# Waiting for every pair of gathers in the attention loop of a four-layer graph network

## The reference

```python
h = (x @ W_att).reshape(n, H, D)
e = a_src[src] + a_dst[dst]
e = jnp.where(e > 0, e, SLOPE * e)
m = segment_max(e, dst)
e = jnp.exp(e - m[dst])
alpha = e / (segment_sum(e, dst)[dst] + SM_EPS)
out = segment_sum(alpha[:, :, None] * h[src], dst)
att_out = out.mean(axis=1) + bias_att
```

## Time and profile before

| | |
|---|---|
| median of the timed runs | 10293.0 us |
| span of the profiled execution | 10335.9 us |
| attention loop, first gather to the first instruction of the next block's gathers | 4321.5 to 7677.2 us |
| POOL busy, whole span | 5859.2 us (57%) |
| DVE busy | 5676.5 us (55%) |
| PE busy | 4876.0 us (47%) |
| gathers at L2099 | 1612, 1588.2 us busy |

### The profile page before, as it was taken

How to read it: one execution, slowest core, us unless ns; L and a number is a source line. 1 busy time by engine, 2 the same in 40 slices (tenths; PEclk the granted TensorE clock), 3 DMA queues, 4 the chain that set the end, 5 groups by cost and what they waited for, 6 DMA issues and landing times. The chain is left out here.

```text
span 10335.9 us, 115065 instructions
## 1 busy us (share of the span) xinstructions
PE 4876.0 (47%) x30691; PEld 3800.3 (37%) x30691; DVE 5676.5 (55%) x16123; ACT 2431.2 (24%) x4069; POOL 5859.2 (57%) x5314
## 2 busy tenths in 40 slices
PE   6888888884666666334444444444467000000000
PEld 3554455442556555234444444444465000000000
DVE  7888888885666666245555555555576212212221
ACT  0111111111333333134444444444453000000000
POOL 5888888884333333444444444444423666666665
PEclk8888888886777877555555555555555555555555
DMA  3333333332000000233333333333331111111111
GB/s 78 35 35 35 35 35 35 35 30 59 20 16 14 15 15 20 46 57 63 64 65 63 63 66 63 64 64 63 64 89 51 46 47 47 46 47 47 46 49 43
DMA packets 927382, 484.76 MB, mean 47 GB/s; under 512 B 828205, under 2 KB 842007, under 8 KB 925218
## 3 DMA queue, kind: packets, MB, share of 16 engines
q0 software_dynamic: 309120, 199.89, 16.7%
q1 hardware_dynamic: 615872, 277.33, 10.0%
q10 hardware_dynamic: 2304, 6.55, 0.2%
HBM read 218.57 MB, written 185.20 MB: 39 GB/s over the span
## 5 line engine op out<-in xcount | busy, mean ns | idle before, releaser
L2099 POOL DMA_INDIRECT tile_rows<-att_row_table,src_by_tile x1612 | 1588.2, 985 | 1676.4 <-ACT tags_l L2117 1181.3
L892 POOL DMA_INDIRECT acc<-val,idx x1240 | 1918.6, 1547 | 416.9 <-issue 372.2
L1142 POOL DMA_INDIRECT rows_l<-relation_table,idx x1612 | 1528.3, 948 | 758.0 <-issue 481.8
L2212 PE MATMUL banks<-rows_l,prob 128*128 128x65 f32 x4032 | 790.2, 376 | 1464.7 <-ACT piece_part L2150 1438.5
L1155 DVE SCALAR_TENSOR_TENSOR run<-run,mask,rows_l 128x64 f32<-128x64 f32 x1612 | 460.8, 286 | 1813.0 <-issue 1332.6
L2212 PEld LDWEIGHTS banks<-rows_l,prob 128*128 128x128 f32 x4032 | 752.3, 287 | 1524.8 <-ACT prob L2144 1233.3
L701 PE MATMUL banks<-part 128*128 128x490 bf16 (+1 forms) x5580 | 1296.6, 392 | 0.0
L1293 POOL DMA_INDIRECT gathered_rows<-h_table,gathered_index x600 | 567.9, 947 | 952.0 <-ACT gathered_index L1403 784.1
L1191 PE MATMUL banks<-run,link 128*128 128x64 f32 x98 | 21.9, 414 | 2299.8 <-PEq L1122 2289.0
L2263 DVE TENSOR_TENSOR banks<-banks,piece_att_dst 128x1024 f32<-128x1024 f32 x252 | 312.2, 1239 | 1436.2 <-remote 1301.6
L1191 PEld LDWEIGHTS banks<-run,link 128*128 128x128 f32 x98 | 21.5, 329 | 2299.5 <-issue 2299.5
(11 more groups left out here) (397 smaller groups left out, 9777.5 us busy)
## 6 DMA issues: line engine op xcount, KB each, us to landing
rows_l<-tile_rows SPq DMA_DIRECT2D x2016, 38.5 KB
piece_sums<-kept_l SPq DMA_DIRECT2D x252, 264.0 KB
running_sums<-run SPq DMA_DIRECT2D x62, 832.0 KB
attr<-in_edge_attr SPq DMA_DIRECT2D x61, 624.0 KB
tile_rows<-att_row_table,src_by_tile POOLq DMA_INDIRECT x1612
rows_l<-relation_table,idx POOLq DMA_INDIRECT x1612
acc<-val,idx POOLq DMA_INDIRECT x1240
gathered_rows<-h_table,gathered_index POOLq DMA_INDIRECT x600
```

The source lines that it names most:

```text
L892: e.indirect_dma_start(acc_d[k], bass.IndirectOffsetOnAxis(ap=idx[h][:, r:r + 1], axis=0), val[h][:, r, :], None, compute_op=ALU.add).then ...
L1142: e.indirect_dma_start(gbuf[h][:, r, :], None, table, bass.IndirectOffsetOnAxis(ap=idx[h][:, r:r + 1], axis=0))\
L2099: e.indirect_dma_start(gathered[:, g % TRING, r, :], None, hx_d, bass.IndirectOffsetOnAxis(ap=src_col[:, t:t + 1], axis=0))\
L2212: last = e.matmul(ps[5 + r // GROUP][:, r % GROUP * W1:(r % GROUP + 1) * W1], prob[u % 2][:, r, :], rows[u][:, r, 0:W1], start=True, stop= ...
```

## The change

POOL still issues the same 1612 gathers in the same order into the same places. Ahead of the third, fifth and seventh gather of a group it now waits until all gathers of this group issued so far have landed; ahead of the first gather of a group it waits until all of the group before have landed. So at most two gathers are under way.

```diff
         ROUNDS = NQ // RING
+        PACE = 2
...
                 @block.gpsimd
                 def _(e):
+                    def tiles_before(g):
+                        return 16 * sum(tiles_of(m) for m in range(g % TSEMS, g, TSEMS))
+
                     def landed(g):
                         e.wait_ge(s_tile[g % TSEMS], 16 * sum(tiles_of(m) for m in range(g % TSEMS, g + 1, TSEMS)))
                         e.sem_inc(s_there, 1)
...
                             landed(g - 2)
                         for r in range(tiles_of(g)):
                             t = g * QUAD + r
+                            if r and r % PACE == 0:
+                                e.wait_ge(s_tile[g % TSEMS], tiles_before(g) + 16 * r)
+                            elif g and not r:
+                                e.wait_ge(s_tile[(g - 1) % TSEMS], tiles_before(g - 1) + 16 * tiles_of(g - 1))
                             e.indirect_dma_start(gathered[:, g % TRING, r, :], None, hx_d,
                                                  bass.IndirectOffsetOnAxis(ap=src_col[:, t:t + 1], axis=0))\
                              .then_inc(s_tile[g % TSEMS], 16)
```

## The result

| | before | after |
|---|---|---|
| median of the timed runs, side by side | 10290.4 us | 10741.0 us (10730.7 to 10756.2, 4 runs) |
| ratio, with its 95% interval | | 1.0439 (1.0426 to 1.0451) |
| span of the profiled execution | 10335.9 us | 10741.1 us |
| first gather of the loop | 4321.5 us | 4301.2 us |
| last gather of the loop | 7558.5 us | 8017.2 us |

The changed kernel is 4.4% slower; the forecast was 10311 us. (The medians differ by 451 us.

What follows compares the result with a forecast made beforehand. The prediction took SP, slowed by POOL's gather bursts, to bound the attention loop. Pairs of 4.10 us add 66 us to the gathers and the end saves 48: +18 on 10293 gives 10311 us, range 10060 to 10780.

Steps and rivals of the forecast that it cites:

- The bound before: Attention loop: SP is late, its register instructions slowed from 37 to a median of 699 ns by POOL's bursts of gathers.
- First to second gather: First term of a pair's period on POOL: 1.25 us from one gather's issue to the next.
- Second gather to landing: Second term of a pair: 2.53 us, from 2.24 quiet for 0.6 of pairs and 2.96 busy for 0.4.
- Landing to the next gather: Third term of a pair: POOL goes on 0.27 us after the landing, between 0.30 less a hidden part and 0.84.
- each wait restarts POOL in full: Rival on POOL's waits: 0.84 us for the third term, pair 4.67, 10770 us; chance 0.15 together with busy landings.
- DVE in the way: Fourth term of a pair: DVE blocks POOL's gather, 0.05 us for a pair, between 0 and 0.24.
- The end of the loop: After the last gather: 68 us from last landing to block end instead of 116.4, 48 us less.
- The range and the side: Whole kernel: 10060 to 10780 us; chances faster 0.36, same 0.14, slower 0.50.
- the offset of span and median: Whole kernel: the timed median was taken 42.9 us below the profiled span, turning 10354 into 10311 us.
- SP slow all the while: Rival in the attention loop: SP stays slow while anything is gathered, +400 to +560 us, 10700 to 10850; chance 0.17.
- a restart of 0.84 us: Rival's third term at POOL's waits: 0.84 us from landing to next gather, 10770 us; chance 0.15 together with busy landings.
- landings mostly busy: Rival on the second term: all landings take 2.96 us, pair 4.53, 10657 us; chance 0.15 together with full restart.

Runs made afterwards that it cites:

- e5: The kernel before, unchanged, run again for its trace on another chip: 8399.6 us, beside 8400.7 for the kernel before in its group.
- e9: Changed kernel with SP's store as 128 runs of 2112 bytes and DVE's scan replaced by a memset: 10339.1 us, 1.0052 of the kernel before.
- e7: Changed kernel with each SP store written as 128 runs of 2112 bytes instead of 1024 of 264: 9504.9 us, 1.1318 of the kernel before.
- e11: Changed kernel, but POOL waits ahead of every gather for the one issued six before: 10289.0 us, 1.0005 of the kernel before.

## Why the prediction was right or wrong

**The bound before: right as read, wrong as a rule.** SP was late, and its slow instructions were the likely cause. e5 shows the same kernel without them, 1085 us shorter in the loop; and in the first trace DVE and ACT have no register instruction over 0.6 us inside the loop, SP alone has them (12% of those at its load). But chip or condition changed between the two runs as well, so this is a comparison, not an experiment on SP alone. And the prediction made a rule of the coincidence with POOL's 1.25 us. On two of the chips the same spacing leaves SP at 37 ns. What sets the condition is open, and so is whether it belongs to the chip. That a stream of one gather in 2.3 us, or in 2.06 (e9), frees SP where it is slow is shown; whether the rate or the number under way does it was not separated.

**First to second gather: right.** 1.26 us, predicted 1.25.

**Second gather to landing: right only up to the last packet.** 2.54 us to the last packet, predicted 2.53. Quiet 2.16 and beside a store 2.99 were close to the 2.24 and 2.96 from the earlier trace rows; the share of pairs beside a store was 239 / 805 = 0.30, not 0.4. But the prediction took the end of the last packet for the landing ("so it landed by about 6049.66"). What POOL waits for is the semaphore, and that rises later: 0.34 us in quiet, 1.12 beside a store, 0.56 on average.

**Landing to the next gather: the size was right, the place was not.** It was put at 0.27 us and counted from the last packet, from where it measures 0.82. Counted from the semaphore it is 0.26, in all pairs. The row that it rested on was a good one: in the earlier trace rows DVE's semaphore rises at 7701.31 and POOL's gather starts at 7701.59, 0.28 us later. So what failed is the step between the two terms: the time from the last packet to the rise of the semaphore was put at nothing, without a reason. It is 0.56 x 806 = 450 us, and the gathers took 479 - 66 = 413 us more than predicted; the rest is small terms of the other sign, above all the 0.05 for DVE, whose blocking is already in the 2.54.

The rival "each wait restarts POOL in full" came close in number, 4.67 us and 10770 against 4.61 and 10741, but by luck. Its 0.84 us stood for a restart, and a restart takes 0.26. In its row ACT's semaphore rises at 6027.12 and POOL goes on at once, 0.03 us later, with another instruction than the gather, the raising of `s_there`:

```profile
L2088 POOLq EVENT_SEMAPHORE  x1: 42/42/42, 6027.1 to 6027.1; - x1
```

The gather starts 0.80 us after that. What fills this time isn't shown; it has nothing to do with a landing.

For the 0.8 us more to the semaphore beside a store, e7 is the proof: with 128 writes in place of 1024 it is gone (0.33 us). By what mechanism the short writes hold the semaphore back isn't shown.

**DVE in the way: undersized.** 0.05 us for a pair was taken, upper end 0.24. 173 gathers were long, with 132 us above the normal 0.94 (0.16 for a pair), and without the scan the kernel gains 165 us (0.20). The Trainium skill, "SBUF — State Buffer", section "Who interferes with whom", has a DVE instruction with two SBUF inputs contend with a GpSimd instruction that reads SBUF. The traces agree: of the 187 gathers of the kernel after that start during the scan 173 are long, of the others none, and with the scan left out none is. By that rule the prediction saw the term near its upper end, 806 x 0.24 = 193 us in all, and 165 lies nearer to that than to the 40 of the sum. The error was hidden by the share of stores, which had been taken too large.

**The end of the loop: right.** 64.9 us from the last gather, predicted 68 from the last landing, that is 70 from the gather.

**The range and the side.** The time lies in the range, on the slower side, which held half of the chances, but 430 us above the point forecast and outside the forecast's own 10230 to 10470. Of the 430 us, 43 are the offset of span and median that did not recur. That the wide range holds the time is in part luck: its upper part stood for rivals (SP slow all the while, a restart of 0.84 us, landings mostly busy) none of which came as described. The side is not luck: the changed kernel is slower in both conditions, by 4.4% where SP is slow and by 18.2% where it isn't.

## What to carry to other kernels

A queue of gathers that is stopped until its own transfers land pays, at every stop, the transfer to its last packet, the time until the semaphore has risen, and the restart (here 2.16 + 0.34 + 0.26 us, against 1.25 us for an issue that isn't stopped). Don't take the last packet for the landing: price the stop from rows in which the landing itself releases the engine. And look for what runs beside it: a store of 1024 short writes added 1.6 us to a stop, the same bytes in 128 longer ones 0.4, and the change of form was worth nothing to the kernel that doesn't stop. A wait placed far enough behind to be met costs nothing (e11). Before pacing an engine to relieve another, see on a second chip that the other is in need of it.

## What the runs showed of the hardware that was not expected

- One and the same kernel takes 10285 to 10293 us in two measurements and 8391 to 8401 us in two others. In the first pair small instructions take about 0.7 or 1.4 us during dense gathers of POOL: 12% of SP's register instructions at its load in the attention loop (over 0.6 us), DVE's register arithmetic (median 0.699) and SP's (median 1.39) in layer 3. In the other pair all of these take 32 to 47 ns. The three chips of the experiments are different ones; that of the first measurement isn't on record, and each chip was met once. Whether the chip or something else sets the condition is open.
- The gathers themselves are the same in both: 0.94 us of work, one every 1.25 us, 3716 and 3721 us for the changed loop.
- POOL's next gather starts 0.26 us after the semaphore of a landing has risen, in all 805 pairs. The semaphore has risen 0.34 us after the last packet in quiet, and 1.12 us after it beside a store of 1024 writes of 264 bytes. That store also makes the last packet 0.8 us later. With 128 writes of 2112 bytes the two are 0.33 and 0.4 us.
- A gather that starts while DVE's scan is running takes up to 2.1 us instead of 0.94; one that is already under way when the scan starts does not become longer (149 of them in the trace after).
